# One kernel's weight preparation in another order, and the steps at the change to attention in an order written out for each engine

## The chip, the cores and the metric

The kernel runs on one core of a Trainium2 chip. The metric is the device time of one execution in microseconds (us). The engines of the core are named as the profile names them: PE (TensorE, the matrix multiplier; PEld is its weight load), DVE (VectorE), ACT (ScalarE), POOL (GpSimd) and SP (SyncE, whose queue issues all the DMAs here). Each engine works through its own list of instructions in order, and the lists meet only at semaphores.

## The reference, cut to what matters

The input x has 16 x 1024 rows of 256 values. Three stages run over it:

```
x = x + 0.5 * ffn(layernorm(x))         # H = 256, inner = 704
x = x + attention(layernorm(x))         # 16 heads, causal linear attention, projection, layernorm
x = x + 0.5 * ffn(layernorm(x))

ffn(x):    h = silu(fp4_linear(x, w_gate)) * fp4_linear(x, w_up);  return fp4_linear(h, w_down)
fp4_linear(x, w): both sides rounded to a grid of eight values per sign,
                  with one scale for each 16 neighbours of a row (largest magnitude / 6)
attention: q, k = elu(.) + 1 + 1e-4;  num = q . cumsum(k v);  den = q . cumsum(k)
           out = num / den @ Wout.T + bout, then layernorm with gamma and beta
```

The weights are quantized on the chip too, once, at the start.

## The kernel before, in words

x is cut into N = 128 tiles of 128 rows, which stay in SBUF (`x_sb`) from the first stage to the last. Each stage is a software pipeline over the tiles: `ffn` (line 653) and `attention` (line 1027) each return one function per engine (`sync_step`, `vector_step`, `gpsimd_step`, `scalar_step`, `tensor_step`), and step i of an engine does that engine's share of several tiles at different depths. In the FFN, step i of PE multiplies tile i by the gate and up weights (L960, "gu(i)" below) and tile i-4 by the down weights (L972, "down(i-4)"); step i of DVE multiplies the two halves (L774), finds block maxima (L785), scales (L778 to L808), makes the rounded values q of the round before (L815), adds the finished tile i-4 to x (L799) and prepares the quotients y (L823); ACT does silu, the statistics and the two roundings (L888, L919); POOL multiplies q by the scales (L843, L851 for x; L867, L868 for h); SP turns the results with transposing DMAs (L753 for x, L759 for h).

In attention, step i of PE computes q, k (L1402) and v (L1415) of tile i+1, transposes k of tile i (L1410), the numerator of tile i-1 (L1435, L1440), the scores of tile i (L1449), its state (L1467) and the projection of tile i-2 (L1476, L1479). DVE's step i has the statistics of tile i+4 (L1159), the features of tile i+1 (L1221), the mask of tile i-1 (L1173); POOL's has the masked keys of tile i (L1273, L1274) and the second half of the split of x of tile i+2 (L1292); SP's places v of tile i+1 (L1131) and turns x of tile i+3 (L1145).

`stages` (line 98) lays the steps of the three stages one behind the other on each engine: most in hardware loops (`in_turns`), the first and last ones unrolled (`in_order`). At the change from the first FFN to attention all engines but for their own offsets follow one scheme: FFN step 125, attention step -4, FFN step 126, attention step -3, and so on in turn up to FFN step 133. At the change to the second FFN each engine has a list of its own (`to_ffn_1`).

The weights' preparation is woven into the first steps of the first stage, in an order written out by hand for each engine in `macaron` (line 177 on). For each of the three FFN weights w (0 gate, 1 up, 2 down) there are: `scales` (DVE), `quotients` (POOL, L501), `rounds` (ACT, L601, L603), `values` (DVE, L524 to L526), `upper` (ACT, the float16 part, L534 to L537) and `lower` (DVE, the rest, L543 or L545). `tops` and `powers` find a power of two for each weight through two small products on PE (L560, L564). For gate and up PE turns the parts in eight sets through three PSUM banks (L577); ACT copies the four upper sets (`copies_hi`, L611) and DVE the four lower sets (`copies_lo`, L616); PE's gu(0) waits for all eight. For the down weight SP turns both parts (L586, L587, L592). The attention weights have POOL's `centre` (L1579), DVE's `tops` (L1597 to L1608) and `powers` (L1619 to L1630), ACT's `upper` (L1635, L1637), POOL's `lower` (L1642) and four transposes on SP (L1544). PE runs the second pair of small products (L560, L564 into `ps_prep`) behind gu(0). ACT's `masks` (L1574) copies two causal blocks.

Of the kernel before, what the change touches and what calls it, by code (L numbers as in the profile page):

```python
# [85 lines left out]

def in_turns(eng, step, first, end, turn):

    with eng.Fori(first, end - turn + 1, turn) as i:
# [5 lines left out]
FIRST, DEPTH = 12, 6  # L95


def stages(eng, N, ffn_0, attn, ffn_1, ffn_ahead=6, attn_first=4, attn_ahead=4, attn_turn=ATTN_TURN, change=None):

    first, ahead = FIRST, 4  # L100

    def loop_end(n_ahead, begin, turn):
        return begin + (N - n_ahead - begin) // turn * turn

    in_turns(eng, ffn_0, first, loop_end(ffn_ahead, first, TURN), TURN)
    in_order(eng, ffn_0, loop_end(ffn_ahead, first, TURN), N + DEPTH - 2 * ahead - 1)
    for k in range(2 * ahead + 1):
        ffn_0(eng, N + DEPTH - 2 * ahead - 1 + k, (k + 1) % 2)
        if k - ahead < attn_first:
            attn(eng, k - ahead, k % 2)  # L110
# [16 lines left out]
def macaron(nc, x, wqkv, bqkv, wout, bout, gamma, beta, wg, wu, wd, out):
    B, L, _ = x.shape
    N = B * L // P
# [4 lines left out]
    with ExitStack() as whole:  # L134
# [42 lines left out]
        @block.sync  # L177
        def _(sp):
            ffn_step = of_ffn_0.sync
            in_order(sp, ffn_step, -9, -8)  # L180
# [33 lines left out]
        def _(dve):
            ffn_step = of_ffn_0.vector
            of_ffn.scales(dve, 0)
            of_ffn.scales(dve, 1)
# [42 lines left out]
        def _(pool):  # L260
# [61 lines left out]
        def _(pe):  # L322
# [20 lines left out]
            stages(pe, N, ffn_step, of_attn_steps.tensor, of_ffn_1.tensor, attn_first=3, attn_ahead=1, attn_turn=2, change=to_ffn_1)  # L343
# [1349 lines left out]
```

## Time and profile before

| | us |
|---|---|
| median of 3 runs | 2159.74 |
| lowest and highest run | 2159.51, 2160.04 |
| the profiled execution's own time | 2161.74 |
| its span, first to last instruction | 2159.9 |
| PE busy | 2095.1 |
| DVE busy | 2042.0 |
| ACT busy | 1922.4 |
| POOL busy | 1915.0 |
| mean granted TensorE clock, share of full speed | 0.995 |

The first FFN runs to about 738 us, where PE's last gu ends. Attention follows it, and then the second FFN. The profile's idle time in front of an instruction stands with the instruction that ended it, with the work that released it; a wait of PE is the thing to look for in most of the span, since PE has the least idle time.

### The profile page before, as it was taken

What the parts mean: (1) busy time and instruction counts of PE and PEld (TensorE: products, weight loads), DVE (VectorE), ACT (ScalarE), POOL (GpSimd) and SP (SyncE); (2) the same over time, 40 slices, a digit from 0 to 9 for tenths busy, and PEclk for the clock granted to TensorE, in tenths of its full rate; (3) what the DMA queues carried; (4) which work ended last, traced back from release to release, by engine and by line L of the source; (5) the groups of instructions that cost most, each with busy time, mean ns of one, the idle gap of its engine ahead of it and who ended that gap; (6) DMA issues with size and microseconds to landing.
All of it is one profiled execution on the core that took longest, in us unless ns stands there. A gap on an engine that the chain in (4) does not pass through costs nothing.

```text
span 2159.9 us, 88415 instructions
## 1 busy us (share of the span) xinstructions
PE 2095.1 (97%) x30384; PEld 1509.9 (70%) x30384; DVE 2042.0 (95%) x5231; ACT 1922.4 (89%) x4137; POOL 1915.0 (89%) x3002
## 2 busy tenths in 40 slices
PE   3899999999999999999999999989999999999998
PEld 1566666666666689999999999975666666666665
DVE  7999999999999889999999999989999999999997
ACT  7888888888888799999999999998888888888885
POOL 5899999999999878888888888889999999999996
PEclk9999999999999999999999999999999999999999
DMA  4665555555556432222233222325555555555555
GB/s 104 131 122 115 116 115 115 116 115 115 114 114 115 85 63 62 62 62 62 62 63 62 62 62 62 63 51 90 117 115 115 115 115 115 115 115 114 115 116 117
DMA packets 719840, 208.49 MB, mean 97 GB/s; under 512 B 666400, under 2 KB 719520, under 8 KB 719776
## 3 DMA queue, kind: packets, MB, share of 16 engines
q1 hardware_dynamic: 719776, 207.76, 47.1%
q8 instruction: 26, 0.43, 0.1%
q14 instruction: 38, 0.31, 0.0%
HBM read 20.38 MB, written 16.78 MB: 17 GB/s over the span
## 4 chain that ended last, share of the span: by engine, by line
PE 92%; DVE 4%; issue 2%; ACT 1%; DMA 1%; POOL 1%; SPq 0%; POOLq 0%; DVEq 0%; ACTq 0%
PE ffn_ps_gu L960 40%; PE ffn_ps_down L972 21%; PE attn_ps_qk L1402 8%; PE attn_ps_sc L1449 5%; PE attn_ps_num L1435 4%; PE attn_ps_v_second L1415 4%; PE attn_ps_z L1479 4%; PE attn_ps_num L1440 2%; PE attn_ps_kT_first L1410 1%; PE attn_ps_z L1476 1%; PE attn_ps_kT_first L1467 1%; DVE ffn_per_block L785 1%; DVE ffn_hx L774 0%; DVE ffn_y L823 0%; DMA x_sb<-in_L_ffn_w_up 0%
## 5 line engine op out<-in xcount | busy, mean ns | idle before, releaser
L960 PE MATMUL ffn_ps_gu<-wgu_hi,ffn_xT 128*128 128x512 f16 (+1 forms) x3072 | 739.7, 364 | 13.4 <-DVE ffn_hx L774 6.2
L960 PEld LDWEIGHTS ffn_ps_gu<-wgu_hi,ffn_xT 128*128 128x128 f16 x3072 | 301.3, 98 | 300.2 <-issue 19.3
L960 PE MATMUL ffn_ps_gu<-wgu_lo,ffn_xT 128*128 128x512 f16 (+1 forms) x1536 | 432.0, 363 | 0.0
L867 POOL TENSOR_TENSOR ffn_h_hl<-ffn_q,ffn_h_scale_hi 128x704 f16<-128x704 f16 x256 | 352.4, 1376 | 28.5 <-DVE ffn_q L815 9.2
L888 ACT ACTIVATE ffn_quarter<-ffn_y,offsets 128x960 int16<-128x960 f32 (+2 forms) x264 | 282.4, 1070 | 99.0 <-DVE ffn_y L823 97.0
L972 PE MATMUL ffn_ps_down<-wd_hi,ffn_hT 128*128 128x256 f16 x2816 | 349.3, 273 | 8.9 <-DVE x_sb L799 5.9
L868 POOL TENSOR_TENSOR ffn_h_hl<-ffn_q,ffn_h_scale_lo 128x704 f16<-128x704 f16 x256 | 355.2, 1388 | 0.0
L972 PEld LDWEIGHTS ffn_ps_down<-wd_hi,ffn_hT 128*128 128x128 f16 x2816 | 274.5, 98 | 69.8 <-issue 7.9
L785 DVE TENSOR_REDUCE ffn_per_block<-ffn_hx 128x60 f32<-128x960 f32 (+2 forms) x264 | 298.0, 1129 | 5.4
L823 DVE TENSOR_TENSOR ffn_y<-ffn_hx,ffn_per_block 128x960 f32<-128x960 f32 (+2 forms) x264 | 292.6, 1108 | 0.0
L878 ACT ACTIVATE ffn_silu<-ffn_ps_gu,unscale 128x704 f32<-128x704 f32 x256 | 215.4, 841 | 76.9 <-PE ffn_ps_gu L960 74.9
L919 ACT ACTIVATE ffn_odd<-ffn_quarter,offsets 128x960 f16<-128x960 int16 (+2 forms) x264 | 278.7, 1056 | 1.7 <-POOL ffn_shift L862 1.6
L960 PEld LDWEIGHTS ffn_ps_gu<-wgu_lo,ffn_xT 128*128 128x128 f16 x1536 | 150.9, 98 | 155.8 <-issue 3.3
L774 DVE SCALAR_TENSOR_TENSOR ffn_hx<-ffn_ps_gu,unscale,ffn_silu 128x704 f32<-128x704 f32 x256 | 240.9, 941 | 17.4 <-PE ffn_ps_gu L960 15.6
L843 POOL TENSOR_TENSOR ffn_x_hl<-ffn_q,ffn_x_scale_hi 128x256 f16<-128x256 f16 x256 | 158.1, 618 | 75.2 <-DVE ffn_q L815 61.4
L972 PE MATMUL ffn_ps_down<-wd_lo,ffn_hT 128*128 128x256 f16 x1536 | 209.5, 273 | 0.0
L1402 PE MATMUL attn_ps_qk<-attn_xT,attn_w_hi 128*128 128x128 f16 x2048 | 179.2, 220 | 4.2 <-DVE attn_expo L1221 2.8
L972 PEld LDWEIGHTS ffn_ps_down<-wd_lo,ffn_hT 128*128 128x128 f16 x1536 | 150.3, 98 | 17.4
L851 POOL TENSOR_TENSOR ffn_x_hl<-ffn_q,ffn_x_scale_lo 128x256 f16<-128x256 f16 x256 | 161.4, 630 | 0.0
L1173 DVE TENSOR_TENSOR attn_scores<-attn_ps_sc,attn_causal 128x1024 f32<-128x1024 f32 x128 | 154.4, 1206 | 0.0
L923 ACT ACTIVATE ffn_hx<-x_sb,ffn_shift,ffn_rstd 128x256 f32 (+1 forms) x256 | 149.9, 586 | 0.0
L1402 PEld LDWEIGHTS attn_ps_qk<-attn_xT,attn_w_hi 128*128 128x128 f16 x2048 | 141.7, 98 | 7.9 <-DMA attn_xT<-attn_x_hl 3.8
(186 smaller groups left out, 5254.3 us busy)
## 6 DMA issues: line engine op xcount, KB each, us to landing
x_sb<-in_L_attn_x SPq DMA_DIRECT2D x128, 128.0 KB, 2.4
out<-x_sb SPq DMA_DIRECT2D x128, 128.0 KB, 2.1
attn_v_eo<-attn_v_nat SPq DMA_DIRECT2D x256, 34.0 KB, 1.8
ffn_xT<-ffn_x_hl SPq DMA_TRANSPOSE x256, 2.5
ffn_hT<-ffn_h_hl SPq DMA_TRANSPOSE x256, 3.5
attn_xT<-attn_x_hl SPq DMA_TRANSPOSE x128, 2.4
attn_oT<-attn_o_hl SPq DMA_TRANSPOSE x128, 2.5
x_sb<-in_L_ffn_w_gate SPq DMA_DIRECT2D x2, 352.0 KB, 4.6
```

The costliest lines, as they stand in the source:

```text
L774: nc.vector.scalar_tensor_tensor(hx[par][:, 0:INNER], ps_gu[par][:, INNER:2 * INNER], unscale[:, 1:2], silu[:], ALU.mult, ALU.mult).then_i ...
L785: nc.vector.tensor_reduce(amax[:, blocks_in(front)], blocks(hx[par][:, front]), AXX, ALU.max, apply_absolute_value=True).then_inc(S["amax" ...
L823: nc.vector.tensor_tensor(blocks(y[:, front]), blocks(hx[par][:, front]), over_block(inv[:, at], at.stop - at.start), ALU.mult).then_inc(S ...
L851: nc.gpsimd.tensor_tensor(blocks(x_hl[par][:, D:]), blocks(q[par][:, INNER:]), over_block(x_scale_lo[par][:], XB), ALU.mult).then_inc(S["x ...
L867: nc.gpsimd.tensor_tensor(blocks(h_hl[par][:, 0:INNER]), blocks(q[par][:, 0:INNER]), over_block(h_scale_hi[par][:], HB), ALU.mult)
L868: nc.gpsimd.tensor_tensor(blocks(h_hl[par][:, INNER:]), blocks(q[par][:, 0:INNER]), over_block(h_scale_lo[par][:], HB), ALU.mult).then_inc ...
L878: nc.scalar.activation(silu[:], ps_gu[par][:, 0:INNER], ACT.Silu, scale=unscale[:, 0:1]).then_inc(S["silu"], 1)
L888: nc.scalar.activation(quarter[:, back], y[:, back], ACT.Identity, bias=offsets[:, 0:1], scale=4.0 / HALF_MIN).then_inc(S["quarter"], 1)
L919: nc.scalar.activation(odd[:, back], quarter[:, back], ACT.Identity, bias=offsets[:, 1:2], scale=HALF_MIN / 4.0).then_inc(S["odd"], 1)
L960: last = nc.tensor.matmul(ps_gu[par][:, a:b], xT[par][:, c, :], w[:, k, a:b], start=(n == 0), stop=(n == len(terms) - 1))
L972: last = nc.tensor.matmul(ps_down[:, 0:D], hT[par][:, c, :], w[:, c, :], start=(n == 0), stop=(n == len(terms) - 1))
L1402: last = nc.tensor.matmul(ps_qk[:, col, :], w[:, col, k], aT, start=(n == 0), stop=(n == len(terms) - 1))
```

## The change

Two things are put in another order; nothing is added, removed or resized.

In the weights' preparation, on DVE and ACT:

```diff
@@ DVE
             in_order(dve, ffn_step, -3, -2)
+            of_ffn.lower(dve, 1)
             of_ffn.lower(dve, 0)
-            of_ffn.lower(dve, 1)
+            in_order(dve, ffn_step, -2, -1)
             of_ffn.copies_lo(dve)
-            in_order(dve, ffn_step, -2, -1)
             of_attn.tops(dve)
+            of_ffn.tops(dve, 1)
             in_order(dve, ffn_step, -1, 0)
-            of_ffn.tops(dve, 1)
             of_ffn.powers(dve, 2, 3)
+            of_ffn.values(dve, 2)
             of_attn.take_powers(dve)
             of_attn.powers(dve)
-            of_ffn.values(dve, 2)
             in_order(dve, ffn_step, 0, 1)
             of_ffn.lower(dve, 2)
@@ ACT
-            of_attn.masks(act)
             in_order(act, ffn_step, -6, -4)
...
             of_ffn.copies_hi(act)
-            in_order(act, ffn_step, -2, 0)
+            in_order(act, ffn_step, -2, -1)
+            of_attn.masks(act)
+            in_order(act, ffn_step, -1, 0)
             of_ffn.rounds(act, 2)
             in_order(act, ffn_step, 0, 1)
+            of_ffn.upper(act, 2)
             of_attn.upper(act)
-            of_ffn.upper(act, 2)
             in_order(act, ffn_step, 1, FIRST)
```

At the change to attention `stages` takes a list `to_attn` for each engine but ACT, which keeps the scheme in turn. F is an FFN step, A an attention step; the scheme before is F125, A-4, F126, A-3, F127, A-2, F128, A-1, F129, A0, F130, A1, F131, A2, F132, A3, F133 (PE: F125 to F128, A-1, F129, A0, F130, A1, F131, A2):

```
SP    F124 F125 F126 F127 A-4 A-3 F128 A-2 A-1 F129 A0 F130 A1 F131 A2 F132 F133 A3
DVE   A-4 F124 F125 F126 A-3 F127 F128 A-2 F129 A-1 A0 F130 A1 F131 A2 F132 F133 A3
POOL  F124 F125 A-4 A-3 F126 F127 A-2 F128 A-1 F129 A0 F130 A1 F131 A2 F132 F133 A3
PE    F124 F125 F126 F127 F128 A-1 F129 F130 A0 A1 F131 A2
```

```diff
-    in_order(eng, ffn_0, loop_end(ffn_ahead, first, TURN), N + DEPTH - 2 * ahead - 1)
-    for k in range(2 * ahead + 1):
-        ffn_0(eng, N + DEPTH - 2 * ahead - 1 + k, (k + 1) % 2)
-        if k - ahead < attn_first:
-            attn(eng, k - ahead, k % 2)
+    in_order(eng, ffn_0, loop_end(ffn_ahead, first, TURN), N - 4)
...
+    if to_attn:
+        to_attn(before_attn, attn_at)
```

## Rows read from the trace of the kernel before

**Rows 1.** The page, part 1: busy us, share of the span and instructions.

```profile
PE 2095.1 (97%) x30384; PEld 1509.9 (70%) x30384; DVE 2042.0 (95%) x5231; ACT 1922.4 (89%) x4137; POOL 1915.0 (89%) x3002
```

**Rows 2.** Waits of PE, 0 to 120 us: who for whom, us in total, times, longest.

```profile
PE ffn_ps_down L972 <- DVE x_sb L799: 2.3, 3, 0.9
```

**Rows 3.** Timeline of DVE, 0 to 75 us: start, duration, what, idle time before.

```profile
26.59 3.46 DVE L545 TENSOR_TENSOR x_sb<-x_sb 128x1408 f16<-128x1408 f32 x2
29.98 2.02 DVE L616 COPY wgu_lo<-ps_prep 128x768 f16<-128x768 f16 x4
31.91 1.83 DVE L778 TENSOR_TENSOR ffn_x_scale_lo<-ffn_scale,ffn_x_scale_hi 128x16 f32<-128x16 f32 x1
...
37.69 1.91 DVE L1607 TENSOR_TENSOR attn_of_pair<-x_sb 128x2 f32<-128x2 f32 x1
...
52.89 3.70 DVE L543 TENSOR_TENSOR x_sb<-x_sb 128x1408 f16<-128x1408 f32 x1 [1.91 <-ACT x_sb L535]
...
57.56 1.15 DVE L785 TENSOR_REDUCE ffn_per_block<-ffn_hx 128x60 f32<-128x960 f32 x1
...
64.71 0.54 DVE L815 TENSOR_SCALAR ffn_q<-ffn_odd 128x960 int16<-128x960 int16 x1 [0.20 <-ACT ffn_odd L919]
```

**Rows 4.** Timeline of POOL, 0 to 90 us.

```profile
30.98 2.74 POOL L1579 TENSOR_TENSOR x_sb<-x_sb 128x1530 f32<-128x1530 f32 x1
...
37.00 2.59 POOL L501 TENSOR_TENSOR x_sb<-x_sb 128x1408 f32<-128x1408 f32 x1
...
52.01 5.59 POOL L1642 TENSOR_TENSOR x_sb<-x_sb 128x1536 f16<-128x1536 f32 x2
...
63.60 1.39 POOL L868 TENSOR_TENSOR ffn_h_hl<-ffn_q,ffn_h_scale_lo 128x704 f16<-128x704 f16 x1
```

**Rows 5.** Timeline of PE, 0 to 90 us.

```profile
33.41 1.87 PE L960 MATMUL ffn_ps_gu<-wgu_hi,ffn_xT 128*128 128x512 f16 x4 [1.94 <-DMA ffn_xT<-ffn_x_hl]
...
38.51 0.27 PE L560 MATMUL ps_prep<-ident,x_sb 128*128 128x128 f32 x1
```

**Rows 6.** Timeline of ACT, 0 to 90 us.

```profile
46.97 1.56 ACT L1635 ACTIVATE x_sb<-x_sb 128x1536 f32<-128x1536 f32 x1
...
51.23 1.36 ACT L534 ACTIVATE x_sb<-x_sb 128x1408 f16<-128x1408 f32 x1
```

**Rows 7.** Timeline of PE, 708 to 790 us.

```profile
741.38 1.36 PE L972 MATMUL ffn_ps_down<-wd_hi,ffn_hT 128*128 128x256 f16 x11 [0.88 <-DVE x_sb L799]
...
750.40 0.58 PE L1402 MATMUL attn_ps_qk<-attn_xT,attn_w_hi 128*128 128x128 f16 x4 [2.82 <-DVE attn_expo L1221]
...
757.98 0.39 PE L1402 MATMUL attn_ps_qk<-attn_xT,attn_w_hi 128*128 128x128 f16 x4
```

**Rows 8.** Timeline of SP's queue, 724 to 790 us.

```profile
740.26 1.20 SPq L1145 DMA_TRANSPOSE attn_xT<-attn_x_hl  x1
742.00 1.38 SPq L759 DMA_TRANSPOSE ffn_hT<-ffn_h_hl  x1
747.80 1.19 SPq L1145 DMA_TRANSPOSE attn_xT<-attn_x_hl  x1
749.17 1.39 SPq L759 DMA_TRANSPOSE ffn_hT<-ffn_h_hl  x1
...
753.66 1.74 SPq L1145 DMA_TRANSPOSE attn_xT<-attn_x_hl  x1
```

**Rows 9.** The page, part 6: us from a DMA's issue to its landing.

```profile
ffn_hT<-ffn_h_hl SPq DMA_TRANSPOSE x256, 3.5
attn_xT<-attn_x_hl SPq DMA_TRANSPOSE x128, 2.4
```

**Rows 10.** Timeline of DVE, 708 to 790 us.

```profile
749.50 0.75 DVE L1221 SCALAR_TENSOR_TENSOR attn_expo<-attn_ps_qk,attn_unscale,attn_expo 128x512 f32<-128x512 f32 x1 [3.46 <-ACT attn_expo L1354]
```

**Rows 11.** Timeline of POOL, 715 to 785 us.

```profile
743.29 1.39 POOL L868 TENSOR_TENSOR ffn_h_hl<-ffn_q,ffn_h_scale_lo 128x704 f16<-128x704 f16 x1
...
752.83 0.68 POOL L1292 TENSOR_TENSOR attn_x_hl<-attn_xn,attn_x_hl 128x255 f16<-128x255 f32 x1
```

More of the change, by code:

```diff
@@ L95, with stages @@
 FIRST, DEPTH = 12, 6
-def stages(eng, N, ffn_0, attn, ffn_1, ffn_ahead=6, attn_first=4, attn_ahead=4, attn_turn=ATTN_TURN, change=None):
+def stages(eng, N, ffn_0, attn, ffn_1, ffn_ahead=6, attn_first=4, attn_ahead=4, attn_turn=ATTN_TURN, to_attn=None, change=None):
     first, ahead = FIRST, 4
@@ L105, in stages, with before_attn, attn_at @@
     in_turns(eng, ffn_0, first, loop_end(ffn_ahead, first, TURN), TURN)
-    in_order(eng, ffn_0, loop_end(ffn_ahead, first, TURN), N + DEPTH - 2 * ahead - 1)
-    for k in range(2 * ahead + 1):
-        ffn_0(eng, N + DEPTH - 2 * ahead - 1 + k, (k + 1) % 2)
-        if k - ahead < attn_first:
-            attn(eng, k - ahead, k % 2)
+    in_order(eng, ffn_0, loop_end(ffn_ahead, first, TURN), N - 4)
+    def before_attn(*steps):
+        for k in steps:
+            ffn_0(eng, k, k % 2)
+    def attn_at(i, **inside):
+        attn(eng, i, i % 2, **inside)
+    if to_attn:
+        to_attn(before_attn, attn_at)
+    else:
+        before_attn(N - 4)
+        for k in range(2 * ahead + 1):
+            before_attn(N - 3 + k)
+            if k - ahead < attn_first:
+                attn_at(k - ahead)
     attn_end = loop_end(attn_ahead, attn_first, attn_turn)
     in_turns(eng, attn, attn_first, attn_end, attn_turn)
-    def attn_at(i, **inside):
-        attn(eng, i, i % 2, **inside)
     def ffn_at(*rounds):
@@ L201, in _, with to_attn @@
             of_attn.turned(sp)
+            def to_attn(ffn_at, attn_at):
+                ffn_at(124, 125, 126, 127)
+                attn_at(-4)
+                attn_at(-3)
+                ffn_at(128)
+                attn_at(-2)
+                attn_at(-1)
+                ffn_at(129)
+                attn_at(0)
+                ffn_at(130)
+                attn_at(1)
+                ffn_at(131)
+                attn_at(2)
+                ffn_at(132, 133)
+                attn_at(3)
             def to_ffn_1(attn_at, ffn_at):
@@ L208, in to_ffn_1 @@
                 return 0
-            stages(sp, N, ffn_step, of_attn_steps.sync, of_ffn_1.sync, 9, change=to_ffn_1)
+            stages(sp, N, ffn_step, of_attn_steps.sync, of_ffn_1.sync, 9, to_attn=to_attn, change=to_ffn_1)
             sp.wait_ge(stored, 16 * N)
@@ L241, in _, with to_attn @@
                 ffn_step(dve, 3 + k, (3 + k) % 2)
+            def to_attn(ffn_at, attn_at):
+                attn_at(-4)
+                ffn_at(124, 125, 126)
+                attn_at(-3)
+                ffn_at(127, 128)
+                attn_at(-2)
+                ffn_at(129)
+                attn_at(-1)
+                attn_at(0)
+                ffn_at(130)
+                attn_at(1)
+                ffn_at(131)
+                attn_at(2)
+                ffn_at(132, 133)
+                attn_at(3)
             def to_ffn_1(attn_at, ffn_at):
@@ L255, in to_ffn_1 @@
                 return 2
-            stages(dve, N, ffn_step, of_attn_steps.vector, of_ffn_1.vector, change=to_ffn_1)
+            stages(dve, N, ffn_step, of_attn_steps.vector, of_ffn_1.vector, to_attn=to_attn, change=to_ffn_1)
         @block.gpsimd
@@ L273, in _, with to_attn @@
             in_order(pool, ffn_step, 2, FIRST)
+            def to_attn(ffn_at, attn_at):
+                ffn_at(124, 125)
+                attn_at(-4)
+                attn_at(-3)
+                ffn_at(126, 127)
+                attn_at(-2)
+                ffn_at(128)
+                attn_at(-1)
+                ffn_at(129)
+                attn_at(0)
+                ffn_at(130)
+                attn_at(1)
+                ffn_at(131)
+                attn_at(2)
+                ffn_at(132, 133)
+                attn_at(3)
             def to_ffn_1(attn_at, ffn_at):
@@ L286, in to_ffn_1 @@
                 return 2
-            stages(pool, N, ffn_step, of_attn_steps.gpsimd, of_ffn_1.gpsimd, change=to_ffn_1)
+            stages(pool, N, ffn_step, of_attn_steps.gpsimd, of_ffn_1.gpsimd, to_attn=to_attn, change=to_ffn_1)
         @block.scalar
@@ L334, in _, with to_attn @@
             in_order(pe, ffn_step, 5, FIRST)
+            def to_attn(ffn_at, attn_at):
+                ffn_at(124, 125, 126, 127, 128)
+                attn_at(-1)
+                ffn_at(129, 130)
+                attn_at(0)
+                attn_at(1)
+                ffn_at(131)
+                attn_at(2)
             def to_ffn_1(attn_at, ffn_at):
@@ L341, in to_ffn_1 @@
                 return 1
[L343 removed]
+            stages(pe, N, ffn_step, of_attn_steps.tensor, of_ffn_1.tensor, attn_first=3, attn_ahead=1, attn_turn=2, to_attn=to_attn, change=to_ffn_1)
 @dataclass
```

## The prediction

> **What bounds the kernel now.** I read the page's busy times first [rows 1]: PE is busy for 2095.1 of 2159.9 us, so a change of order can win at most PE's 64.8 idle us and what a low clock adds. Then the waits of PE, to see where these are, and then the timelines of each engine there. Two stretches are touched. In the first, up to about 110 us, DVE is hardly ever idle, and PE still waits three times behind 70 us, 2.3 us in all, for the addition L799 [rows 2]. So until there DVE's list sets the time, and a shift of DVE's list by some amount is a shift of the end by that amount. In the second, at the change to attention, the waits are PE's own: 0.88 us before down(124), and 2.82 us before qk of tile 1 (L1402), for the features L1221 [rows 7].
>
> DVE does the same work in any order, so for the first stretch only its idle time and its stalls count. A stall is an instruction that takes longer than it should. Three stand out [rows 3]: L778 on 16 columns takes 1.83 us, and ends just where POOL's L1579, begun at 30.98 for 2.74, ends [rows 4]; L1607 on two columns takes 1.91 and ends with POOL's L501 (37.00 + 2.59); L543 takes 3.70, while L545, the same operation on as many columns, takes 3.46 for two, and the first of POOL's two L1642 began at 52.01. Against some 0.1, 0.15 and 1.7 us undisturbed they lose 1.7, 1.75 and 2.0. L815 is of this kind: issued at 64.71 it ends 0.3 us behind POOL's L868, which ended at 64.99. The copies L616 beside L1579 run on (0.5 us each). So one engine waits for the other's whole instruction. With the 1.91 idle before L543 and 0.3 in small pieces, DVE loses 7.65 us between 30 and 61 us.
>
> The Trainium skill has this as a rule ("SBUF — State Buffer", "Who interferes with whom"): VectorE and GpSimd share a port pair that is held for a whole instruction, and a VectorE instruction with two SBUF inputs or in a two-port mode has to have it, a reduction or one with a PSUM input not. The trace agrees (L778 1.83 us, L616 undisturbed). Without that rule I would price the head at the removed 1.91 us of idle time alone, and have 1.9 us faster there.
>
> **The head, DVE.** Until 26.59 nothing differs: ACT's masks took 0.5 us at the start in front of a wait for x and weights, and fall later into an idle time of 3 us. The two L545 change places, which costs nothing (both inputs are there by 26.4), and end at 30.05. Then:
> - FFN step -2 comes before the copies. L778 waits for POOL's L851 (until 30.55: 0.5), L785 to L805 follow, and L815 is reached at 31.6, while L1579 holds from 30.98 to 33.72 [rows 4]. It stalls 2.1 us. Before, the copies lay beside L1579 and only L778 stalled. L823 ends at 34.25, and the four copies at 36.3 instead of 32.0.
> - PE's gu(0) needs the copies: it starts at 36.3 instead of 33.41, 2.9 later. It took 5.1 us (33.41 to 38.51 [rows 5]), its first products at the lower of the two clock levels (0.47 us each, where it later takes 0.22) behind idle time; I take the same, so it ends at 41.4, and L560, which stands behind it, at 41.7.
> - attention's tops: L1607 reaches POOL at 39.1, when L501 (now from 36.65) is nearly through: stall 0.3 instead of 1.75. DVE is done at 39.6.
> - ffn.tops(1) now stands directly behind, and waits for L560 [rows 5]: 2.2 us idle, from 39.6 to 41.75. Step -1, which stood there as cover (1.4 us), is now behind it. What is queued behind that wait is all of DVE's list.
> - tops, step -1, powers, values(2) and the attention powers are 8.0 us of work with 0.3 of stalls; L514 no longer waits. Step 0 starts at 48.6 to 49.0 instead of 46.55.
> - ACT: upper(2) stands before attention's upper, so hi of the down weight is ready some 4.3 us (46.97 to 51.23 [rows 6]) earlier in ACT's list, at about 50.5, and lower(2) no longer waits: the 1.91 us go. POOL's L1642 comes as much later as ACT's list moves: silu(1), 1.7 us of upper(2) and the first half of upper (3.0 us) end near 53.5, L1642 would start at 54.2.
> - DVE's step 0 ends at 53.4. POOL's L851 holds to 53.9; lower(2) then runs undisturbed to 55.6, before L1642, so the stall of 2.0 goes. But L1642 (2.7 us for its first part) then holds from 55.8, and L778 of step 1 waits for it: 1.9. L785 follows at 58.6 instead of 57.56 [rows 3].
>
> Sum of DVE's losses after: 0.5 + 2.1 + 0.3 + 2.2 + 0.3 + 0.5 + 1.9 = 7.8, and 0.1 to 0.9 for silu(1), which ACT ends at 54.9 to 55.7. Against 7.65 the head is 0.2 to 1.0 slower; I take 1.0, the end at which POOL's small instructions are held up by values(2) and so ACT's step 0. Bounds: every collision and wait of the new list gone, the head is limited by PE, whose waits up to 110 us are 2.3 and small ones: -2.6. gu(0) wholly at the lower level (7.1 us, twice 3.57) and one more collision of 0.9: +3.9. SP's transposes of the down weight (six of 1.3 us) come behind the turn of x of tile 3, which is 1.9 us later; gu(4) is then about 1 us later than now, inside PE's slack of 2.6.
>
> **The change to attention.** Before, SP turned x of tile 1 (747.80) before h of tile 126 (749.17), though h was split at 744.68 (L868, 743.29 + 1.39 [rows 11]); down(126) stood behind attention step 0 on PE. After:
> - SP issues h(125) first, but not before down(123) has freed its buffer (742.0 before, and 740.6 at the earliest). xT(0), at 740.26 before [rows 8], goes to 742.0 and lands 2.4 us later [rows 9], at 744.5. PE's qk(0), at 743.24, waits 1.3 us. Nobody behind it suffers: ACT's v of tile 0 is held by POOL's memsets until 747.05 anyway.
> - down(125) ends at 748.4, and DVE adds tile 125 at once (L799 until 748.9; it stood behind L1221). h(126) is issued at 744.8 and lands by 748.3 (3.5 us [rows 9]). So down(126), 1.86 us, runs from 749.0 to 750.9, inside the wait of 2.82 [rows 7]. L1221 starts at 749.7 instead of 749.50 [rows 10].
> - Attention step 0 on PE starts at 750.95 instead of 750.40. Its end is set by ACT's k of tile 0 (L1363), now 754.7: state products until 755.05.
> - Step 1 then needs x of tile 2: POOL's L1292 ends at 753.51 [rows 11], SP issues at 753.66 [rows 8], and it lands at 756.1. qk(2) starts at 756.15 instead of 757.98 [rows 7].
> That is 1.8 us faster, and down(127) and step 2 follow as before. The wait of 0.88 stays: L799 stands behind the same L774 and L785. Attention step -4's statistics, 0.6 us, move ahead of F124 on DVE and are gone ahead of F126, where DVE catches up and waits for PE's gu again; POOL's step -3 goes into 1.3 us in which it waits for q. Both cost nothing with that cover, and 0.6 and 1.4 us without it. Bounds: 0 if h(126) or the addition comes late, so that down(126) delays step 0 by as much as it saves; 3.2 if x of tile 2 comes 1.4 earlier and no clock is lost.
>
> **Sum.** +1.0 - 1.8 = -0.8 us. The profiled execution takes 2161.74 us, so 2160.9; it is 2.0 above the median of 2159.74, against which the comparison is made: 2158.9. All loops are the same.
>
> **The rivals.**
> - The head wins as it was meant (faster): the collision of L815 with L1579 is avoided or shorter and tops(1) finds PE done, so that the idle 1.91 and the stall 2.0 are simply gone. PE caps this at 2.6: -2.6 - 1.8 = -4.4, 2155.3 us. For it: the two losses are real rows. Against it: L1579's place at 30.98 follows from POOL's own list, and gu(0) cannot start without the copies.
> - PE's late first product (slower): gu(0) at the lower clock level throughout. DVE stands behind it for tops(1), price 2.0, from any gu(0) longer than 3.3 us (39.6 - 36.3) on, one us for one us. +3.0 - 1.8 = +1.2, 2160.9 us. For it: PE is idle for 2.7 us just before. Against: it reached full speed after 2.5 us last time.
> - The transition wins nothing: h(126) lands late, because turns of x and v share the queue. +1.0 - 0 = +1.0, 2160.7 us.
>
> **How the numbers follow.** 0.48 for my forecast, 0.22 for the first rival, 0.18 for the second (a third of it with a further collision and over 4.3 us slower), 0.12 for the third. A measurement of this kernel can tell 0.2% (4.3 us) from no change. About three quarters of the first rival lie beyond it, the others hardly: faster 0.17, same 0.76, slower 0.07. Range for 8 in 10: from the first rival at 2155.0 to 2162.5, where both stretches are near their slow bounds.
>
> **What would show it.** Right: L815 of about 2.3 us near 31.6; gu(0) near 36.3; an idle time of about 2 us on DVE before L506 near 41; L543 of 1.7 us with no wait; L778 of some 2 us behind it; down(126) directly before qk(1), and no 2.82 us wait. Wrong: L815 short, gu(0) before 35, or DVE not idle before L506, where the head wins; qk(2) no earlier relative to down(123), where the transition doesn't; an end more than 4.3 us off on either side.

## The result, and the profile after

The changed kernel takes 2163.93 us (median of 17 runs, 2160.78 to 2167.11), the kernel before 2160.69 in the same session (17 runs, 2157.51 to 2162.96): ratio 1.0014 [1.0008, 1.0020], 3.2 us slower, where 0.8 us faster was forecast; 2163.93 lies outside the stated range, which ended at 2162.5. A second session gave 1.0021 [1.0011, 1.0030]. The profiled execution took 2166.76 us, span 2164.7; 2.8 above the median. Lines of the changed kernel are those of before plus 68.

The head, in the changed kernel. DVE's timeline (start, duration, what, idle time before), which answers to [rows 3]:

```profile
31.90 2.32 DVE L883 TENSOR_SCALAR ffn_q<-ffn_odd 128x256 int16<-128x256 int16 x1
...
42.94 0.29 DVE L574 TENSOR_REDUCE x_sb<-ps_prep 128x1 f32<-128x128 f32 x1 [3.18 <-PE ps_prep L628]
...
52.81 0.22 DVE L883 TENSOR_SCALAR ffn_q<-ffn_odd 128x256 int16<-128x256 int16 x1
...
54.14 1.62 DVE L611 TENSOR_TENSOR x_sb<-x_sb 128x1408 f16<-128x1408 f32 x1
56.27 0.95 DVE L842 SCALAR_TENSOR_TENSOR ffn_hx<-ffn_ps_gu,unscale,ffn_silu 128x704 f32<-128x704 f32 x1 [0.51 <-ACT ffn_silu L946]
57.14 2.67 DVE L846 TENSOR_TENSOR ffn_x_scale_lo<-ffn_scale,ffn_x_scale_hi 128x16 f32<-128x16 f32 x1
59.73 1.15 DVE L853 TENSOR_REDUCE ffn_per_block<-ffn_hx 128x60 f32<-128x960 f32 x1
```

POOL's timeline, which answers to [rows 4]:

```profile
31.40 2.74 POOL L1647 TENSOR_TENSOR x_sb<-x_sb 128x1530 f32<-128x1530 f32 x1
...
46.92 1.75 POOL L930 TENSOR_SCALAR ffn_shift<-ffn_neg_mean,ffn_rstd 128x1 f32<-128x1 f32 x1
...
54.20 2.04 POOL L919 TENSOR_TENSOR ffn_x_hl<-ffn_q,ffn_x_scale_lo 128x256 f16<-128x256 f16 x1
...
56.68 4.20 POOL L1710 TENSOR_TENSOR x_sb<-x_sb 128x1536 f16<-128x1536 f32 x2
```

Up to DVE's step 0 it reads as predicted: L883 stalls behind L1647, DVE idles for PE's L628, L846 of step 1 stalls behind L1710. What is new is the third line of POOL: L919, the second half of the split of x of tile 3, takes 2.04 us instead of 0.62, beside DVE's lower(2) (L611). The next engine in that chain is SP. Its queue of the kernel before, and then of the kernel after:

```profile
51.73 1.19 SPq L753 DMA_TRANSPOSE ffn_xT<-ffn_x_hl  x1
52.98 1.28 SPq L586 DMA_TRANSPOSE wd_hi<-x_sb  x1
...
58.27 2.62 SPq L592 DMA_TRANSPOSE wd_lo<-x_sb  x2
61.02 0.50 SPq L741 DMA_DIRECT2D x_sb<-in_L_attn_x  x1
62.39 1.24 SPq L753 DMA_TRANSPOSE ffn_xT<-ffn_x_hl  x1
```

```profile
56.41 1.19 SPq L821 DMA_TRANSPOSE ffn_xT<-ffn_x_hl  x1
57.65 2.42 SPq L654 DMA_TRANSPOSE wd_hi<-x_sb  x1
...
64.09 2.62 SPq L660 DMA_TRANSPOSE wd_lo<-x_sb  x2
66.84 0.50 SPq L809 DMA_DIRECT2D x_sb<-in_L_attn_x  x1
67.95 1.34 SPq L821 DMA_TRANSPOSE ffn_xT<-ffn_x_hl  x1
```

In both, six turns of the down weight and a load of x stand between the turn of x of tile 3 (x(3) from here on) and that of tile 4, almost back to back: 10.7 us before, 11.5 after. So x(4) is as late as x(3) was, and more: the first turn of the down weight took 2.42 us, where the others take 1.28. Such a slow turn comes and goes between profiles (2.19 in the second one of this kernel, none in e1 below), and its cause was not found. POOL's split of x(4) was through at 63.96, long before the turn at 67.95. PE, before and then after, at gu(3) and gu(4):

```profile
57.59 1.86 PE L960 MATMUL ffn_ps_gu<-wgu_hi,ffn_xT 128*128 128x512 f16 x4 [6.22 <-DVE ffn_hx L774]
...
64.94 1.02 PE L960 MATMUL ffn_ps_gu<-wgu_hi,ffn_xT 128*128 128x512 f16 x4 [2.22 <-issue]
```

```profile
60.72 1.89 PE L1028 MATMUL ffn_ps_gu<-wgu_hi,ffn_xT 128*128 128x512 f16 x4 [4.41 <-DMA ffn_xT<-ffn_x_hl]
...
70.65 1.86 PE L1028 MATMUL ffn_ps_gu<-wgu_hi,ffn_xT 128*128 128x512 f16 x4 [3.77 <-issue]
```

Before, gu(3) waited for DVE's step 1, which frees its PSUM; after, it waits for the turn of x(3). gu(4) starts 5.7 us late, behind 3.77 us of idle time, and then runs at the lower level: 1.86 us for four products that took 1.02. The profile names no releaser for its wait ("issue"). That it is the turn of x(4) is read from three things: the turn lands 2.5 us behind its issue, gu(4) starts 2.5 to 2.8 us behind that issue in all the profiles in which it had to wait at all, and in five of them (e1, e6, e7, e8, e9) the profile does name the turn. The granted clock by stretch (PE busy, PEld, DVE, ACT, POOL, PEclk, DMA share, GB/s), after, and then before:

```profile
45.00:65.00 20.00, 12.39 (x43) 4.82 (x42) 19.11 (x47) 15.14 (x28) 14.11 (x17) 0.76 0.33 57
65.00:85.00 20.00, 16.23 (x84) 8.68 (x83) 16.61 (x41) 15.30 (x35) 16.60 (x23) 0.81 0.63 127
```

```profile
45.00:65.00 20.00, 11.46 (x46) 4.71 (x45) 17.74 (x34) 16.95 (x33) 12.89 (x15) 0.78 0.41 82
65.00:85.00 20.00, 19.21 (x118) 11.21 (x119) 19.88 (x50) 17.49 (x40) 19.16 (x27) 1.00 0.64 118
```

DVE is busy for 16.6 of the 20 us from 65 to 85, where it had 19.9: it now waits for PE, 3.0 us in all.

POOL's rows show that the later of two instructions waits for the whole of the earlier one: L611 at 54.14, L919 at 54.20, ended 0.5 us behind it. The lead of 0.06 us is not chance. Both instructions hang on DVE's q of that step (L883 at 52.81): what stands behind the step on DVE starts 1.33 us after it, POOL's L919 1.39 us after it, in the second profile 1.34 and 1.39. The kernel before has the same order. DVE, and then POOL, of the kernel before:

```profile
49.55 0.22 DVE L815 TENSOR_SCALAR ffn_q<-ffn_odd 128x256 int16<-128x256 int16 x1
...
61.11 0.94 DVE L774 SCALAR_TENSOR_TENSOR ffn_hx<-ffn_ps_gu,unscale,ffn_silu 128x704 f32<-128x704 f32 x1
```

```profile
50.94 0.62 POOL L851 TENSOR_TENSOR ffn_x_hl<-ffn_q,ffn_x_scale_lo 128x256 f16<-128x256 f16 x1
...
61.17 0.62 POOL L851 TENSOR_TENSOR ffn_x_hl<-ffn_q,ffn_x_scale_lo 128x256 f16<-128x256 f16 x1
```

At 50.94 POOL is 1.39 us behind q again, and DVE has nothing to do, since lower(2) still waits for ACT. At 61.17 DVE's next instruction is 0.06 us ahead of POOL's, as in the changed kernel, and does no harm: L774 reads one input from PSUM, and the split takes its 0.62 us. The Trainium skill ("SBUF — State Buffer", "Who interferes with whom") has the same rule, that whoever issues first has the port pair that the two share for a whole instruction and the other is blocked; by that rule, the trace agrees (2.04 us).

The change to attention, PE's timeline, which answers to [rows 7]:

```profile
748.51 1.36 PE L1040 MATMUL ffn_ps_down<-wd_hi,ffn_hT 128*128 128x256 f16 x11 [1.04 <-DVE x_sb L867]
...
752.33 0.38 PE L1470 MATMUL attn_ps_qk<-attn_xT,attn_w_hi 128*128 128x128 f16 x4 [1.80 <-DMA attn_xT<-attn_x_hl]
...
757.01 1.36 PE L1040 MATMUL ffn_ps_down<-wd_hi,ffn_hT 128*128 128x256 f16 x11 [0.67 <-DVE x_sb L867]
...
758.86 0.39 PE L1470 MATMUL attn_ps_qk<-attn_xT,attn_w_hi 128*128 128x128 f16 x4
```

The wait of 2.82 us is gone and down(126) stands directly before qk(1), as predicted; instead qk(0) waits 1.80. From down(123) to qk(3) it takes 24.49 us, 25.88 before, 1.4 us less. But the two profiles were not at the same clock there (columns as above; before, after, and e6_copies, which has the new lists too):

```profile
742.00:758.00 16.00, 12.52 (x158) 10.84 (x157) 6.28 (x16) 13.05 (x27) 12.93 (x23) 0.89 0.44 85
742.00:758.00 16.00, 12.49 (x110) 9.27 (x108) 10.99 (x33) 11.87 (x24) 13.35 (x19) 1.00 0.57 90
742.00:758.00 16.00, 12.92 (x145) 10.61 (x145) 5.93 (x18) 11.40 (x22) 11.32 (x19) 0.89 0.40 76
```

All the profiles, us from down(123) to qk(3), sorted by the clock of that stretch (e13 and e16, with one exchange more, follow at the end of the experiments):

| | granted clock 0.89 | granted clock 1.00 |
|---|---|---|
| the scheme in turn | before 25.88, e4 26.13 | e3 24.68, e1 25.44, e15 25.47 |
| the new lists | e6 26.16, e7 26.14, e8 26.13 | after 24.49, again 24.50, e2 24.51, e5 24.59, e9 24.53, e10 24.49, e12 24.51 |

So at the same clock the lists gain 0.2 to 1.0 us at the full clock, and nothing at the lower one. The 1.4 us compare a stretch at the full clock with one that was partly at the lower level.

A ledger of the head and of the change, this profile and the second one of the same kernel (e14_again), both against the profile of before. Starts of PE's products, read from its timeline:

| | before | after | after, again |
|---|---|---|---|
| x(3) turned by SP | 51.73 | 56.41 | 55.13 |
| x(4) turned by SP | 62.39 | 67.95 | 66.44 |
| gu(4), and its length | 64.94, 3.7 | 70.65, 6.3 | 69.14, 5.4 |
| gu(5) | 70.83 | 78.64 (+7.8) | 76.25 (+5.4) |
| gu(12) | 111.53 | 118.49 (+7.0) | 115.75 (+4.2) |
| down(123) | 738.49 | 745.45 (+7.0) | 742.71 (+4.2) |
| qk(3) | 764.37 | 769.94 (+5.6) | 767.21 (+2.8) |
| span | 2159.9 | 2164.7 (+4.8) | 2163.2 (+3.3) |

The loss is all there at gu(5). Two spreads limit what a single profile says. The kernels whose preparation is as before have gu(12) at 111.53 (before), 112.43 (e2) and 112.92 (e13), so +4.2 and +7.0 are +2.8 to +7.0 against all of them. And behind the change to attention the profiles drift against each other by up to 2.5 us in loops that are the same.

### The profile page after: what moved, and what is told of

It reads as the page before. It is cut to its first block, busy times and chain, and to the rows that moved or that the text cites. A ratio compares the mean times of both kernels' runs of the same rounds, so it can differ in the third digit from the quotient of the medians.

```text
span 2164.7 us, 88416 instructions
## 1 busy us (share of the span) xinstructions
PE 2098.7 (97%) x30384; PEld 1510.1 (70%) x30384; DVE 2046.0 (95%) x5231; ACT 1920.5 (89%) x4137; POOL 1912.1 (88%) x3002
## 4 chain that ended last, share of the span: by engine, by line
PE 93%; DVE 3%; issue 1%; DMA 1%; SPq 1%; ACT 1%; POOL 0%; POOLq 0%; DVEq 0%; ACTq 0%
PE ffn_ps_gu L1028 41%; PE ffn_ps_down L1040 21%; PE attn_ps_qk L1470 8%; PE attn_ps_sc L1517 5%; PE attn_ps_num L1503 4%; PE attn_ps_v_second L1483 4%; PE attn_ps_z L1547 4%; PE attn_ps_num L1508 2%; PE attn_ps_kT_first L1478 1%; PE attn_ps_z L1544 1%; PE attn_ps_kT_first L1535 1%; DVE ffn_per_block L853 0%; DVE ffn_hx L842 0%; DMA x_sb<-in_L_ffn_w_up 0%; PE attn_ps_v_second L1535 0%
## 5 line engine op out<-in xcount | busy, mean ns | idle before, releaser
L853 DVE TENSOR_REDUCE ffn_per_block<-ffn_hx 128x60 f32<-128x960 f32 (+2 forms) x264 | 298.0, 1129 | 5.4
L919 POOL TENSOR_TENSOR ffn_x_hl<-ffn_q,ffn_x_scale_lo 128x256 f16<-128x256 f16 x256 | 162.3, 634 | 0.0
```

What stands on the lines that cost most here:

```text
L853: nc.vector.tensor_reduce(amax[:, blocks_in(front)], blocks(hx[par][:, front]), AXX, ALU.max, apply_absolute_value=True).then_inc(S["amax" ...
L919: nc.gpsimd.tensor_tensor(blocks(x_hl[par][:, D:]), blocks(q[par][:, INNER:]), over_block(x_scale_lo[par][:], XB), ALU.mult).then_inc(S["x ...
```

## The experiments

My theory (A; up to e5 the expectations have only its second half, the row of transposes in front of x(4)): PE is late because POOL's split of x(3) waits behind lower(2), so SP starts its row of transposes late and x(4) comes late. Rivals: DVE's losses in the head set the time, as the prediction had it; or PE's low clock behind idle time does, above all in gu(0).

**e1_head** and **e2_change**: each half of the change alone.

```
e1:  new order of the preparation; stages() and its loop as before
e2:  preparation as before; to_attn lists for SP, DVE, POOL, PE
```

> The new weight preparation alone, with the old scheme at the change to attention. Theory A (PE's late start: x of tile 4 is turned only behind the six turns of the down weight, so gu(4) and all of PE behind it are late): the trace of the changed kernel has gu(12) 7.0 us later and the change to attention 1.4 us shorter, so this one is about 1.4 us slower than the changed kernel, 4 to 5 us slower than before (ratio about 1.002). Theory B (DVE's losses alone set the head, as forecast): +1.0 us, ratio 1.0005. Theory C (the change to attention is what costs): no slower than before.

> The lists at the change to attention alone, with the old weight preparation. Theories A and B: down(126) fills PE's wait, 1.4 us faster than before as between the two traces (forecast 1.8), ratio 0.9993. Theory C: slower than before by 3 us. qk(3) should start 1.4 to 1.8 us earlier behind down(123) than the 25.9 us (738.49 to 764.37) of before.

e1: 2164.50 us against 2160.75, ratio 1.0014 [1.0005, 1.0024]. e2: 2159.94, 0.9994 [0.9985, 1.0003]. The loss is the head's: 3.8 us, a little under A's 4 to 5, and the forecast's +1.0 (B) lies at the lower end of its interval. The lists gain 0.8 by the medians, too little to tell from none. That fits the table above better than the 1.4 us of the two first profiles.

**e3_act** and **e4_dve**: the head by engine.

```
e3, ACT:  upper(2), copies_hi ahead of attention's upper; masks later
e4, DVE:  lower(1), lower(0), step -2, copies_lo, tops, tops(1), step -1, ..., values(2)
```

> ACT's part of the new preparation alone on the kernel before (masks later, upper(2) ahead of attention's upper). lower(2) should no longer wait 1.91 us nor stall 2.0, but L778 behind it stalls some 1.7 to 2.7 on POOL's L1642. Theory A: x of tile 4 is bound by SP's six turns, which end at 61.5 either way, so gu(4) moves by less than 1 us: 0 to 1 us faster. Theory B: DVE's losses fall by about 2 us, 2 us faster. If ACT's part is what costs, slower.

> DVE's part of the new preparation alone on the kernel before. Theory A: the start of gu(0) moves to 36.5 and DVE waits 2 to 3 us for the product behind it, and with ACT's old order lower(2) and the turns of the down weight come another 3 to 4 us later: 5 to 8 us slower. Theory B: DVE's losses rise by 1 us and the wait of 1.91 comes back, 2 to 4 us slower.

e3: 2162.71, 1.0009 [1.0000, 1.0018]. e4: 2162.92, 1.0011 [1.0002, 1.0020]. Both expectations of e3 missed: faster was expected by A and by B, and it came out slower. e4 is 2.2 us slower, which B had (2 to 4) and A had not (5 to 8). The trace of e3 shows that the wait itself had a use. DVE of e3, and then POOL and SP of e3 (its lines are those of before plus 1):

```profile
51.33 1.61 DVE L544 TENSOR_TENSOR x_sb<-x_sb 128x1408 f16<-128x1408 f32 x1
54.06 0.95 DVE L775 SCALAR_TENSOR_TENSOR ffn_hx<-ffn_ps_gu,unscale,ffn_silu 128x704 f32<-128x704 f32 x1 [1.12 <-ACT ffn_silu L879]
```

```profile
51.38 2.04 POOL L852 TENSOR_TENSOR ffn_x_hl<-ffn_q,ffn_x_scale_lo 128x256 f16<-128x256 f16 x1
```

```profile
53.59 1.19 SPq L754 DMA_TRANSPOSE ffn_xT<-ffn_x_hl  x1
...
63.99 1.19 SPq L754 DMA_TRANSPOSE ffn_xT<-ffn_x_hl  x1
```

DVE begins step 1 at 54.06, 2.5 us earlier than before (56.51), and the kernel is 2.0 us slower by the medians. (The profiled execution, 2160.28 us, was the fastest of the eleven; its gu(12) is at 113.32, 0.4 to 1.8 us later than in the kernels with the old preparation.) So an earlier DVE does not make this kernel faster. Before, DVE's L543 waited 1.91 us for ACT until 52.89 [rows 3], and by then POOL's split (until 51.56) was through. The removed wait had kept DVE off POOL. In e4 the split takes 0.62 us but starts 1.6 us later, with DVE's list; x(3) is turned at 53.32 and x(4) at 63.98, the same lateness handed on by SP. gu(4) starts at 66.51 as in e3 (66.52), but behind 2.0 us of idle time instead of 4.0, and takes 3.7 us instead of 6.4: the lateness and the clock behind it are two costs.

**e5_sp**, **e6_copies**, **e7_tops**, **e9_lower**: one edit each on the changed kernel.

```
e5, SP:   turn_hi ahead of in_order(sp, ffn_step, 1, 2)
e6, DVE:  copies_lo ahead of in_order(dve, ffn_step, -2, -1)
e7, DVE:  tops(dve, 1) behind in_order(dve, ffn_step, -1, 0)
e9, DVE:  lower(dve, 2) behind in_order(dve, ffn_step, 1, 2)
```

> The changed kernel with one edit: SP issues the four turns of the down weight's upper part ahead of x of tile 3 instead of behind it. Theory A (PE late through SP's six turns): in the changed kernel's trace SP stood idle from 48.8 to 56.4 us, the four turns fit in there, x of tile 4 goes out when it is split (64.0) instead of at 67.95, gu(4) starts near 66.7 instead of 70.65 and right behind gu(3), so at full clock: 3 to 5 us faster than the changed kernel (2163.9), about 2160. Theory B (DVE's losses, 7.8 us, set the head): DVE's list is as before, no gain over the changed kernel, 2163 to 2164.

> The changed kernel with DVE's four copies back ahead of FFN step -2. The stall on POOL's L1579 goes from q (2.3 us) back to the small L846 (1.8 us), gu(0) starts at 33.8 instead of 36.5 and ends near 39, so DVE's wait of 3.2 us for the product behind it shrinks to none. DVE is 3 us earlier from there. Theory A: x of tile 3, held up by lower(2), comes 3 us earlier too, and gu(4) with it: 2 to 3 us faster than the changed kernel. Theory B: 3 us faster as well. If only the clock of the head matters: less than 1 us.

> The changed kernel with DVE's tops(1) back behind FFN step -1, which then covers 1.4 us of the 3.2 us wait for the product behind gu(0). Theories A and B: 1.0 to 1.4 us faster than the changed kernel. If the wait there costs nothing: the same.

> The changed kernel with DVE's lower(2) one FFN step later, so that it can no longer hold up POOL's second part of x of tile 3 (2.04 us instead of 0.62 in the changed kernel's trace). Theory A: POOL's L919 takes 0.62 again, x of tile 3 goes to SP 1.4 us earlier, the upper turns of the down weight too; the lower ones must wait for lower(2), near 61, and x of tile 4 goes out near 65 instead of 68: 1.5 to 3 us faster than the changed kernel. Theory B: DVE does the same work, L846 no longer meets L1710 behind lower(2) but lower(2) may: no gain, within 1 us.

| kernel | x(4) turned | gu(4) | gu(5) | gu(12) | us (before: 2161.01) | ratio |
|---|---|---|---|---|---|---|
| e5_sp | 63.52 | 66.05 | 71.68 | 113.59 | 2162.32 | 1.0007 [0.9998, 1.0016] |
| e6_copies | 63.72 | 66.40 | 74.16 | 112.11 | 2162.34 | 1.0008 [0.9998, 1.0017] |
| e7_tops | 64.23 | 66.96 | 73.87 | 111.82 | 2163.11 | 1.0007 [0.9998, 1.0016] |
| e9_lower | 65.73 | 68.54 | 76.30 | 115.56 | 2164.93 | 1.0021 [1.0012, 1.0030] |

Each of the first three turns x(4) earlier than either profile of the changed kernel (67.95, 66.44). Their ratios are lower than its 1.0014 and 1.0021, with intervals that include 1 and overlap its own: a part of the loss, at most. e5 was to win 3 to 5 us and won 1.6 by the medians, which is more than B allowed and half of what A said. Its rows say where the rest is: gu(5) is only 0.9 us late, but gu(12) is 0.7 to 2.1 us later than with the old preparation, and on the way PE waits for DVE's additions (L867). DVE begins step 2 at 62.24, 1.1 us later than before (61.11). That part is DVE's own list, of about the size that the prediction gave it (1.0). e6 (2 to 3 us expected, 1.6 measured) and e7 (1.0 to 1.4, and 0.8) fell short too; both their profiles are among the three that lost 1.6 us to the clock at the change to attention. e9 missed. POOL and SP of e9 (before's lines plus 69) show why:

```profile
52.65 0.62 POOL L920 TENSOR_TENSOR ffn_x_hl<-ffn_q,ffn_x_scale_lo 128x256 f16<-128x256 f16 x1
...
60.38 2.03 POOL L920 TENSOR_TENSOR ffn_x_hl<-ffn_q,ffn_x_scale_lo 128x256 f16<-128x256 f16 x1
```

```profile
59.73 1.28 SPq L656 DMA_TRANSPOSE wd_hi<-x_sb  x1
61.96 2.54 SPq L661 DMA_TRANSPOSE wd_lo<-x_sb  x2
...
65.73 1.19 SPq L822 DMA_TRANSPOSE ffn_xT<-ffn_x_hl  x1
```

The split of x(3) is free (0.62 us), but lower(2), one step later at 60.32, now holds up the split of x(4), and SP's last two turns wait for lower(2) itself, which ends at 61.93. It is these two turns that make x(4) late: its split ended at 62.41, 3.3 us before its turn. So e9 shows that the collision moves with lower(2), and says nothing of what it costs.

**e14_again**: the changed kernel unaltered. **e12_sp_copies**: e5 and e6 together. **e8_act_change**: the changed kernel with DVE's preparation as before.

> The changed kernel once more, unaltered, to see how much of its first profile is the kernel's and how much the execution's. Theory A (the order of the preparation makes POOL give up the port to VectorE's lower(2), x of tile 3 comes late, SP turns the down weights first, x of tile 4 comes late): again the transpose of x of tile 3 on SP after 54.5 us (before: 51.73), that of tile 4 after 65 (before: 62.39), gu(5) at 76 to 79, and the time 2.5 to 4 us over the kernel before. Rival (the first profile was an unlucky one, and its 7 us at gu(12) were low clock by chance): x of tile 4 as in the first profile, but gu(12) at 113 to 115, and the time within 1.5 us of the kernel before.

> The changed kernel with both edits that helped when made alone: VectorE's copies_lo back ahead of step -2, and SP's four turn_hi ahead of the turn of x of tile 3. Theory A: turn_hi alone moved x of tile 4 on SP from 67.95 to 63.52, the copies alone to 63.72; together to about 62.4, where POOL's split sets it, gu(4) at 65 to 66 at the high clock, gu(12) at 111.0 to 112.5, and the time 2159.0 to 2161.0, below the kernel before by what the transition gains (0 to 1.4). Rival (gu(0) at the low clock and VectorE's stalls cost by themselves, whatever x of tile 4 does): no better than either alone, 2162.0 to 2163.5.

> The changed kernel with VectorE's preparation as it was before (so ScalarE's new order and the lists at the change to attention). ScalarE's part alone cost 2.0 us, the lists alone gained 0.8. Theory A: the two add up, 2161.5 to 2162.5. Rival (ScalarE's part is harmless and its 2.0 us were the spread of one session): 2159.5 to 2160.5.

Against 2160.22 in that session: e14 2164.99, 1.0021 [1.0011, 1.0030]; e12 2160.04, 0.9999 [0.9990, 1.0008]; e8 2160.92, 1.0006 [0.9997, 1.0015]. e8 fell between its two expectations and its interval reaches into both, so it decides nothing. e12 against e14 is the main test: 5.0 us apart on one chip, and their intervals do not meet; A gave e12's time as 2159.0 to 2161.0, the rival 2162.0 to 2163.5. But e12 takes two things away at once, since with the copies first DVE begins step 0 at 47.35, 1.2 and 2.5 us earlier than in the two profiles of the changed kernel. It shows that the two together are the loss, not how it divides. SP, POOL and PE of e12:

```profile
53.52 1.28 SPq L655 DMA_TRANSPOSE wd_hi<-x_sb  x1
...
55.62 1.19 SPq L821 DMA_TRANSPOSE ffn_xT<-ffn_x_hl  x1
56.86 2.61 SPq L660 DMA_TRANSPOSE wd_lo<-x_sb  x2
...
62.11 1.31 SPq L821 DMA_TRANSPOSE ffn_xT<-ffn_x_hl  x1
```

```profile
51.74 2.04 POOL L919 TENSOR_TENSOR ffn_x_hl<-ffn_q,ffn_x_scale_lo 128x256 f16<-128x256 f16 x1
```

```profile
64.80 1.02 PE L1028 MATMUL ffn_ps_gu<-wgu_hi,ffn_xT 128*128 128x512 f16 x4 [0.26 <-issue]
```

POOL's split is held up all the same, and x(3) is even turned at 55.62. But the four turns that used to follow it are out of the way, x(4) is turned at 62.11, gu(4) starts at 64.80 and runs at the higher level (1.02 us). gu(0) ran at the lower level for most of its time in this profile (33.68 to 40.34, 6.7 us), and the loss is gone all the same. The stall by itself is not the loss either: it costs only with the turns that SP has to do behind it.

**e15_sp_alone**, the control: SP's edit on the kernel before. **e10_best**: SP's edit on e8.

```
e15, e10, SP:  turn_hi ahead of in_order(sp, ffn_step, 1, 2)
```

> The kernel before with SP's four turn_hi ahead of the turn of x of tile 3, nothing else: the control for the run that brought the changed kernel level. Theory A (the turns of the down weight hurt only where x of tile 3 is late; before, POOL's split of x of tile 4 ends at 61.8 and its turn went out at 62.39): at most 0.6 us to win, gu(4) at 64.3 to 65.2, time 2159.5 to 2160.8. Rival (early turns of the down weight are a gain of their own in any order, so that the changed kernel's cure says nothing of the cause of its loss): 2156.5 to 2158.5.

> ScalarE's new order and the lists, VectorE's preparation as before, and SP's four turn_hi ahead of the turn of x of tile 3. With SP's old order this gave 2160.9, gu(4) at 67.98. Theory A: x of tile 4 goes out at 61.5 to 62.0 instead of 65.44, gu(4) at 64.3 to 65 at the high clock, time 1 to 2 us below, 2159.0 to 2160.0. Rival (VectorE, not the transposes, sets gu(5) to gu(12)): 2160.5 to 2161.3.

Against 2160.83: e15 2161.76, 1.0004 [0.9995, 1.0013]; e10 2159.88, 0.9995 [0.9986, 1.0004]. The edit gains nothing by itself. My expectation of e15 missed in detail: before, ACT has the upper part of the down weight ready only at 52.8, so turn_hi waited and held x(3) back to 59.23, and gu(4) came at 67.56 instead of 64.3 to 65.2. gu(5) came 2.2 us late and gu(12) at 111.43, 0.1 early: PE's waits for DVE's additions absorbed it. In e10 gu(4) came at 63.97 and at the higher level, as expected, and gu(12) at 108.75 (e8: 112.69). So SP's edit alone was run on three kernels: on the changed one the ratio went from 1.0014 and 1.0021 to 1.0007, on e8 from 1.0006 to 0.9995, and on the kernel before, where x(3) was not late, from 1 to 1.0004. Each pair's intervals overlap, so by time the two gains are a direction and no more; by the starts of PE's products they are clear.

**e13_xT0** and **e16_all**: one exchange in SP's list at the change, on e2 and on e12.

```
-ffn_at(124, 125, 126, 127)
+ffn_at(124, 125, 126)
 attn_at(-4)
 attn_at(-3)
-ffn_at(128)
+ffn_at(127, 128)
```

> The lists at the change alone, with one exchange more: on SP attention's step -3 (the turn of x of tile 0) ahead of feed-forward step 127 (the turn of h of tile 125) as before the change, step 128 still ahead of step -2. In every profile with the new lists qk(0) waits 1.8 to 2.0 us for that turn. Theory T (SP's order makes it late): the turn goes out at about 741.6 instead of 743.45, qk(0) waits 0.1 to 0.3, and the time is 1 to 2 us below that of the lists alone, 2158.0 to 2159.3. Rival (POOL's split is late too, or the h of tile 125 becomes the wait): qk(0) still waits over 1 us or down(125) waits as much, time within 0.7 of the lists alone (2159.3 to 2160.6).

> The changed kernel with all three edits that helped or were level: copies_lo back ahead of step -2, SP's turn_hi ahead of the turn of x of tile 3, and attention's step -3 ahead of feed-forward step 127 on SP. The first two gave 2160.0. Theory A with T: qk(0) no longer waits 1.97 us, but qk(2) and down(125) wait 1.7 together as where the exchange was made alone, so 0.3 to 1.0 us below: 2159.0 to 2159.8. Rival (the exchange is worth its whole 1.9 here): 2158.0 to 2158.5; other rival (nothing): 2160.0 to 2160.6.

e13: 2158.96, 0.9992 [0.9983, 1.0001]; e16: 2159.32 against 2160.83, 0.9993 [0.9984, 1.0002]. PE's waits in e13:

```profile
747.45 1.38 PE L1039 MATMUL ffn_ps_down<-wd_hi,ffn_hT 128*128 128x256 f16 x11 [0.53 <-DMA ffn_hT<-ffn_h_hl]
750.15 1.36 PE L1039 MATMUL ffn_ps_down<-wd_hi,ffn_hT 128*128 128x256 f16 x11 [0.67 <-DVE x_sb L866]
...
757.57 0.40 PE L1469 MATMUL attn_ps_qk<-attn_xT,attn_w_hi 128*128 128x128 f16 x4 [1.17 <-DMA attn_xT<-attn_x_hl]
```

qk(0) does not wait any more, but down(125) waits 0.53 us for its h and qk(2) 1.17 for its x: 24.11 us from down(123) to qk(3) in both kernels, 24.51 without the exchange, all at the full clock. Both times fall where T had them; the waits that came in place of the old one are those of its rival. Neither kernel is shown to beat the one before; their intervals reach past 1.

## Why the prediction was wrong

- **The order of two instructions, read the wrong way round.** "POOL's L851 holds to 53.9; lower(2) then runs undisturbed to 55.6" is the step that failed. By its own numbers POOL was first by 0.1 us (53.9 less 0.62, against the end of DVE's step 0 at 53.4), a tie that it took for an order. The order stands in the trace of the kernel before: there too DVE's next instruction starts 0.06 us ahead of POOL's (61.11 and 61.17), because both follow DVE's q. In the two profiles DVE's L611 started at 54.14 and 52.87, POOL's L919 at 54.20 and 52.92, and POOL waited. The split cost 2.04 us instead of 0.62. The prediction counted what POOL does to DVE and nothing that DVE does to POOL.
- **SP's queue.** The turn of x of tile 3 was priced at 1.9 us late and gu(4) at "about 1 us later than now". The second number does not follow from the first: behind a queue without gaps gu(4) is late by the same 1.9, even had the split not been held up. The turn was 4.7 and 3.4 us late in the two profiles: the 1.9, the 1.4 of the split, and in the first another 1.3 of gu(0), which took 6.3 us there and 5.1 in the second (ends 42.80 and 41.52). gu(4) followed at +5.7 and +4.2. SP had been busy from 51.73 to 61.5 almost without a gap, so nothing of the lateness could go; the slow turn of the down weight added most of another 0.9 and 0.6.
- **The clock.** gu(4), behind 3.8 and 4.5 us of idle time, took 6.3 and 5.4 us for 3.7: another 2.6 and 1.7. The prediction looked for the low clock in gu(0) alone.
- **"Inside PE's slack of 2.6."** The size was right. Behind gu(5) PE needs 5.42 us a step where it waits for nothing, so gu(12) comes no earlier than 37.9 us behind gu(5). Before, it came 2.8 us later than that, which is the slack. In e6, e7 and e8, with gu(5) at +3.3, +3.0 and +3.9, it is gone, and gu(12) stands at 37.9 us exactly. With gu(5) at +5.4 and +7.8 it could not be enough. gu(12) then came another 1.5 and 1.9 us later, behind waits for the additions of DVE, which had waited 1.7 and 3.0 us for PE's gu and was late as well.
- **DVE's sum.** Losses 7.8 against 7.65 were forecast, the head 1.0 slower. L853 of step 1 came at 59.73 and in the second profile at 58.44, for a forecast 58.6; the idle time before it was 3.18 and 1.92 for 2.2, and L846 took 2.67 in both, a loss of some 2.5 instead of 1.9. So the steps were right, in the second profile to 0.2 us, and that kernel was still 4.2 us late at gu(12). The frame was not: "until there DVE's list sets the time" left out the list of SP.
- **The transition.** -1.8 forecast, -1.4 read from both profiles and e2 against the one profile of before. Of this 0.2 to 1.0 is the lists' gain at the full clock; the rest comes from the profile of before, which was at the lower level in qk(1) and from which the forecast was made. qk(0) waited 1.8 to 2.0 us for a forecast 1.3, as the turn of h(125) ahead of it went out later than assumed. In e6, e7 and e8 PE was at the lower level from qk(0) on, behind that wait, and the gain was gone.
- **The rivals.** The slower one, gu(0) at the lower level, did occur for most of gu(0) in the first profile and cost there what it said, one us for one us: 1.3 us later at the end of gu(0), 1.3 at the turn of x(3). In the second profile gu(0) took 5.1 us (before: 5.3), and the kernel was still 4.2 us late at gu(12): it is an addition, not the cause. The faster one had the idle 1.91 us simply gone. In e3 it is, and that is what costs.

So +4.2 to +7.0 at gu(12) in place of +1.0, less what the lists gain, stands against a median 3.2 to 4.8 us slower. How much of the head's loss an execution has depends on how long the low clock lasts in gu(0), gu(1) to gu(4); that spread was seen and not taken apart. How the loss divides between SP's queue and DVE's own list is open too: e5 leaves 0.7 to 2.1 us at gu(12) to DVE, within the spread of the profiles. And the collision itself was never taken away alone. In before, e2, e4, e13 and e15 both splits are free, but there lower(2) waits for ACT; with ACT's new order only e9 freed the split of x(3), and it held up SP's last two turns instead.

## What to carry to other kernels

Before removing a wait, ask what it keeps apart: an engine that starts earlier asks for shared things earlier, and the one to be priced is the other engine's instruction and the queue behind that. In a queue without gaps count every transfer between the late one and the next one that the critical engine needs; the lateness is handed on whole. A near tie between two engines is worth reading from the trace before: if both follow the same instruction, its order is fixed. And an idle time put in front of TensorE can be charged again at its clock, so compare two profiles of a stretch only with their granted clocks beside them.

## What the hardware showed

- A lead of 0.05 to 0.06 us decided which of the two went first, the same way in all twelve profiles in which lower(2) stood directly behind DVE's step (2.03 to 2.04 us for the split each time), and small instructions wait as long as large ones: L930 on one column took 1.75 us beside L594's 1.62, and 0.26 alone.
- The same wait in front of qk(0), 1.8 to 2.0 us, was followed by the full clock in seven profiles (1.00 from 742 to 758 us) and by the lower level in three (0.89), which cost 1.6 us.
- The same loops of attention, 120 steps of 5.38 us, differed by up to 2.5 us between profiles (644.0 us from qk(3) to qk(123) in e13, 646.5 in e12); nothing in the change touches them.
